# A fused four-layer kernel: the last block's second half in two quarters, their products on VectorE

## The reference

```python
x = x + L0(x)   # Haar transform, every level times one gate: v + gate * v for this kernel
x = x + L1(x)   # h_t = tanh(x_t Wx + b + h_{t-1} Wh), over 512 tokens
x = x + L2(x)   # below
x = x + L3(x)   # x + x @ (base + x_a x_b^T), x_a and x_b of rank 8 per batch row

# L2
forget_gate, input_gate = sigmoid(x Wf + bf), sigmoid(x Wi + bi)
gate_sum = forget_gate + input_gate + EPS
forget_norm, input_norm = forget_gate / gate_sum, input_gate / gate_sum
new_info = input_norm * (x Wh + bh)
log_cumprod = cumsum(log(forget_norm + EPS), axis=1)
scaling = exp(log_cumprod[:, -1:] - padded[:, :-1])      # product of the later forget factors
hidden = cumsum(scaling * new_info, axis=1) + exp(log_cumprod) * initial_hidden
```

## Time and profile before

| what | us |
|---|---|
| median of 3 runs | 1376.03 (1373.47 to 1377.22) |
| the profiled execution's own time | 1375.73 |
| its span in the profile | 1373.9 |
| TensorE busy | 1341.6 (98%) |
| VectorE busy | 1045.2 (76%) |
| GpSimd busy | 825.7 (60%) |
| ScalarE busy | 794.3 (58%) |

### The profile page before, as it was taken

How to read it: one execution, slowest core, us unless ns; L and a number is a source line. 1 busy time by engine, 2 the same in 40 slices (tenths; PEclk the granted TensorE clock), 3 DMA queues, 4 the chain that set the end, 5 groups by cost and what they waited for, 6 DMA issues and landing times. The chain is left out here.

```text
span 1373.9 us, 51170 instructions
## 1 busy us (share of the span) xinstructions
PE 1341.6 (98%) x21246; PEld 899.0 (65%) x21246; DVE 1045.2 (76%) x2694; ACT 794.3 (58%) x2733; POOL 825.7 (60%) x695
## 2 busy tenths in 40 slices
PE   8999999999999999999999999999999998998998
PEld 6656666666666666666666666666666645766776
DVE  5856878787878787878787878778777798894652
ACT  4387566666666666666666666666656543333342
POOL 3255656565756565656565656575647666775773
PEclk9999999999999999999999999999999999999999
DMA  9761141413131322232322314130305445677773
GB/s 372 279 256 37 26 72 25 72 28 69 33 64 35 62 41 57 41 56 42 56 51 47 60 38 70 27 56 10 61 6 110 113 89 158 227 210 237 265 250 118
DMA packets 304168, 134.74 MB, mean 98 GB/s; under 512 B 272945, under 2 KB 275121, under 8 KB 300738
## 3 DMA queue, kind: packets, MB, share of 16 engines
q1 hardware_dynamic: 303472, 131.10, 37.2%
q10 hardware_dynamic: 466, 0.38, 0.1%
HBM read 80.07 MB, written 51.38 MB: 96 GB/s over the span
## 5 line engine op out<-in xcount | busy, mean ns | idle before, releaser
L524 PEld LDWEIGHTS recb<-hs,scanS 128*128 128x128 f16 x16352 | 476.9, 96 | 137.1 <-DVE hs L1614 133.6
L524 PE MATMUL recb<-hs,scanS 128*128 128x32 f16 x16352 | 488.1, 176 | 4.3 <-DVE hs L1614 3.3
L792 ACT ACTIVATE hs<-pre 128x64 f16<-128x64 f32 x512 | 131.2, 256 | 387.9 <-DVE pre L1600 382.3
L1406 DVE RECIPROCAL gates<-gates 128x64 f32<-128x64 f32 x480 | 244.9, 531 | 0.0
L1600 DVE TENSOR_REDUCE pre<-recb 128x64 f32<-128x128 f32 x511 | 148.9, 291 | 123.1 <-PE recb L524 100.5
L1614 DVE TENSOR_TENSOR hs<-konst,hs 128x64 f16<-128x64 f32 x512 | 114.1, 223 | 105.8 <-ACT konst L793 105.4
L1114 POOL TENSOR_SCALAR hbuf<-hbuf,sup 128x512 f32<-128x512 f32 (+2 forms) x61 | 94.2, 1545 | 131.9 <-ACT hbuf L797 131.9
L1122 POOL TENSOR_TENSOR gates<-gates 128x512 f32<-128x512 f32 x60 | 76.4, 1273 | 87.7 <-DVE gates L1406 87.7
L797 ACT ACTIVATE hbuf<-pre 128x64 f32<-128x64 f32 x512 | 122.7, 240 | 0.0
L1256 POOL TENSOR_TENSOR x3l<-xt,x3h 128x512 fp32r<-128x512 f32 x64 | 83.7, 1309 | 57.9 <-ACT x3h L1004 57.9
L787 ACT ACTIVATE recb<-xw 128x128 f32<-128x128 f32 x447 | 116.9, 261 | 0.0
(11 more groups left out here) (283 smaller groups left out, 2882.3 us busy)
## 6 DMA issues: line engine op xcount, KB each, us to landing
xt<-in_x SPq DMA_DIRECT2D x64, 256.0 KB, 4.0
out<-scanS SPq DMA_DIRECT2D x63, 256.0 KB, 2.6
n_d<-nst SPq DMA_DIRECT2D x60, 256.0 KB, 3.1
x_d<-xt SPq DMA_DIRECT2D x60, 256.0 KB, 4.3
xt<-x_d SPq DMA_DIRECT2D x28, 512.0 KB, 5.7
stage<-in_w SPq DMA_DIRECT2D x11, 1024.0 KB, 7.0
xw<-n_d SPq DMA_DIRECT2D x14, 512.0 KB, 5.4
late<-n_d SPq DMA_DIRECT2D x14, 512.0 KB, 5.6
```

The source lines that it names most:

```text
L524: last = nc.tensor.matmul(sums[t % 2][:, m].rearrange("p a b -> p (a b)"), w[:, k, m * P:(m + 1) * P], hs[:, k].rearrange("p a b -> p (a b ...
L792: nc.scalar.activation(hs[:, :, 0, :], pre[t % 2][:], ACT.Tanh, scale=unscale).then_inc(s_h, 1)
L1406: nc.vector.reciprocal(piece, piece).then_inc(s_r, n)
```

## The change

1. Half 1 becomes two quarters: group 1 is batch rows 8 to 11, group 2 rows 12 to 15 (`group`, `side`), with instructions 128 elements wide (132 for scans). The reciprocal is one instruction for each.
2. The forget product and the product of share and suffix of both quarters are done by VectorE, directly behind the reciprocal and behind the scans. GpSimd keeps them for half 0 and keeps `add_half`.
3. The pieces stand at regular places: for group e + 1 and chunk m, shares after `hidden(8 + 16 e + 2 m)`, scans three places later, info six places later.
4. `spill_half` of group 2 stands at the end of b = 9, and the first load of row 12 behind the stores of row 9, with a wait for these spills.
5. ScalarE copies the whole candidate (512 wide, into xt's buffer of block 14) out of its bank before `last_X(3)`, and `last_info` reads it there for all groups. TensorE's first batch row waits for this copy alone and no longer for `last_info` of half 0.
6. The order at the start of the closing stage changes: `hidden(0)` and `hidden(1)` ahead of `following(2, 0)` and `decay_half(3, 0)`; `x3_low` interleaved with `times_n`; `x3_high` of row 1 ahead of `put_out(0)`.
7. `JOINED` is 2 instead of 1.
8. In block 1, at steps 9 and 10, two maxima (`greatest_x`) stand behind the step's `hs` instruction instead of ahead of it.

```diff
-JOINED = 1
+JOINED = 2
...
-REST = {5: [("sum", 0)], 6: [("rest", 0)], 7: [("sum", 1)], 8: [("rest", 1)], 9: [("sum", 2)], ...
+FIRST_REST = 8
+
+def rest_at(first, gap=2):
+
+    return {FIRST_REST + 16 * e + first + gap * m: (m, e + 1) for e in range(2) for m in range(C)}
+
+REST_SHARES, REST_SCANS, REST_INFO = rest_at(0), rest_at(3), rest_at(6)
+REST_FORGET, REST_TOTAL = rest_at(1), rest_at(4)
+REST_LATER = rest_at(7)
...
-        group = [slice(h * HALF, (h + 1) * HALF) for h in range(2)]
+        group = [slice(0, HALF), slice(HALF, HALF + B // 4), slice(HALF + B // 4, B)]
+        side = [slice(g.start * TS, g.stop * TS) for g in group]
...
                     elif m == 0:
                         pe.wait_ge(s_cb, t + 1)
-                        pe.wait_ge(s_n, final(t, 0))
...
             for k in range(C, SLOTS):
                 hidden(k)
...
+                if k in REST_SHARES:
+                    m, h = REST_SHARES[k]
+                    shares_of(m, h)
...
+                    nc.vector.tensor_tensor(flast[m][:, side[h]], flast[m][:, side[h]], rlast[m][:, side[h]], ALU.mult).then_inc(s_fr, 1)
+                if k in REST_SCANS:
...
+                    later(m, h)
+                    decay_half(m, h)
...
+                    nc.vector.tensor_tensor(share, share, sfx[:, m % 2, group[h], 1:SEG], ALU.mult).then_inc(s_vs, 1)
+                if k in REST_INFO:
+                    following(*REST_INFO[k])
+                    last_info(*REST_INFO[k])
```

More of the change, by code:

```diff
@@ L275, in rank, with scanned @@
             return h * C + m + 1
+        def scanned(m, h):
+            return 4 * C * (NBLK - 1) + rank(m, h) + (m + 1 if h == 0 else C)
         def final(m, h):
@@ L477, in _ @@
             for b in range(B):
-                if b + 2 < B and b + 2 != HALF:
+                if b + 2 < B and b + 2 not in (HALF, HALF + B // 4):
                     load("n", b + 2, 0)
@@ L1056, in _ @@
             last_n(2)
+            candidate(3)
             last_X(3)
-            candidate(3)
             x3_high(2)
@@ L1061, in _ @@
             x3_high(3)
+            x3_high(C)
             y_high(0)
-            x3_high(C)
+            x3_high(C + 1)
+            x3_high(C + 2)
             for t in range(NT):
                 put_out(0, t)
+            x3_high(C + 3)
             def high_and_rest(k):
@@ L1246, in times_n @@
                     loaded(pool, "n", k)
-                pool.wait_ge(s_F, rank(m, b // HALF))
+                pool.wait_ge(s_F, rank(m, next(h for h in range(3) if b < group[h].stop)))
                 part = nin[b % 2][:, m, 0:blocks * TS].rearrange("p (q t) -> p q t", t=TS)
@@ L1297, in _ @@
             add_half(2, 0)
-            times_n(2)
             x3_low(0)
             later_share(3, 0)
+            times_n(2)
+            x3_low(1)
             add_half(3, 0)
             times_n(3)
-            x3_low(1)
+            times_n(C)
             x3_low(2)
+            times_n(C + 1)
             x3_low(3)
-            for k in range(C, C + 3):
-                times_n(k)
+            times_n(C + 2)
             x3_low(C)
@@ L1631, in _ @@
                         factors(C - 1)
+                    if j == 1 and t in (9, 10):
+                        greatest_x(3, t - 7)
                     if j == 1 and t == 8:
@@ L1706, in later @@
                     dve.wait_ge(s_t, C * (last - 2) + m + 3)
-                for e in range(2):
-                    part = slice(h * HALF + e * B // 4, h * HALF + (e + 1) * B // 4)
+                for e in range(0, group[h].stop - group[h].start, B // 4):
+                    part = slice(group[h].start + e, group[h].start + e + B // 4)
                     dst, src = (s[:, part, :].rearrange("p b t -> p (b t)")[:, ::-1] for s in (sfx[:, m % 2], gst[:, m]))
@@ L1771, in _ @@
             decay_half(2, 0)
-            following(2, 0)
             hidden(0)
             later(3, 0)
+            last_info(1, 0)
+            following(2, 0)
+            hidden(1)
             decay_half(3, 0)
-            last_info(1, 0)
-            hidden(1)
+            last_info(2, 0)
             following(3, 0)
-            last_info(2, 0)
             hidden(2)
```

99 lines of the change are left out of this document (37 added, 62 removed).

## The result

The changed kernel takes 1379.89 us (median of 13 runs, 1377.01 to 1382.08), the kernel before 1376.06 beside it (13 runs): ratio 1.0024, 95% interval 1.0016 to 1.0033. By this ratio it is slower by about 3.3 us, 0.24%; the medians differ by 3.8. The forecast was 1376.5, "same". The profiled execution took 1380.9 us with a span of 1379.1, 5.2 more than the span of before.

A forecast was written before the change was run, and what follows sets the result against it. VectorE was taken to hold TensorE's rows 1 to 5, with about 23 us to win. Gains were given back: E8 0.5 us later and row 12 0.3 later, 0.8 on 1375.73, gave 1376.5 us; range 1363 to 1386.

The forecast's parts named there:

- x: Excess time of each VectorE instruction with two SBUF inputs, waiting for GpSimd's current instruction: 0.44 us whatever its width.
- E8: Start of batch row 8's low-rank matmuls on TensorE; forecast 1279.0 us against 1278.5 before, 0.5 later.
- Row 12's load: Row 12's first load waits in the queue as row 8's did; 0.3 us taken; rival of 4.6 + 2.9, chance 0.07.
- E9: Start of batch row 9's low-rank matmuls on TensorE; the prediction gave it no time of its own.
- the cheap lock: Rival: GpSimd is found busy less often, x below 0.36, measurably faster, 1366 us at x = 0.25; chance 0.32.
- The start: Closing stage's start: TensorE's third and fourth bank wait for ScalarE's candidate copies, winning 2.1 of 3.5 us.
- E0: Start of batch row 0's low-rank matmuls on TensorE; forecast 1153.7 us, before 1155.78.
- Row 3 and after: TensorE's rows 3 to 8 wait for VectorE: `hidden(15)` at 1191.2, `hidden(31)` at 1250.8, `hidden(35)` at 1267.7.
- E3: Start of batch row 3's low-rank matmuls on TensorE; forecast 1205.4 us, before 1204.6.
- E7: Start of batch row 7's low-rank matmuls on TensorE; forecast 1265.0 us, before 1265.73.
- The waits: Sign: TensorE waits about 10 us before row 3 and 5 before row 7, each with some 5 us of low clock behind.
- No wait near row 8's first load: Sign: that load's lateness lies under TensorE's 5.4 us wait for `hidden(31)`; before, it made TensorE wait 4.56 us.

The follow-up runs named there:

- row12: Changed kernel with the second quarter's stores one batch row earlier and row 12's first load ahead of factor loads and output stores in SyncE's queue: 1373.26 us, ratio 0.9982.
- pool_prod: Changed kernel with both products of the quarters on GpSimd, scans four and infos seven places behind the shares: 1373.44 us, ratio 0.9981 to the kernel before.
- pool_j8_cand: Changed kernel with quarter products on GpSimd, row 8's and 12's first loads ahead, `JOINED = 8`, and ScalarE's fourth candidate copy right behind the third: 1365.77 us, ratio 0.9929.
- spread: Changed kernel with the second quarter's VectorE work at every third place instead of every second: 1377.13 us, ratio 1.0004 to the kernel before.
- both_rows: row12 with row 8's first load also ahead of factor loads and stores in SyncE's queue: 1372.92 us, ratio 0.9972 to the kernel before.
- twice: row12 with eight extra VectorE products, each multiplying a reciprocal with itself, result unread: 1377.95 us, ratio 1.0020 to the kernel before.

## Why the prediction came out as it did

The number lay 3.4 us low, inside the range; the direction was right within the bound of 0.3%, but on its upper side. That it came so near is in part luck. The lock's price x was measured at 0.33, below the 0.36 where the prediction has the change measurably faster; by the sum's own steepness, 5.6 us for 0.1, it would have given about 1370. Steps that ran late, row 12 and the main loop made up for it. The sum ended at E8 0.5 later and row 12 0.3 later. Measured: E8 1.1 earlier from the memset, row 12 3.9 later, 0.17 in block 1. Times below are less 2.4 us, the main loop's part, which the sum counted at nothing; in the profiles the kernels with the new main loop reach the mark 1.7 us later on average.

- **Row 12's load: the term that failed.** "I take 0.3 us there, between 0 and 4.6 + 2.9" became 3.9, over half of the upper bound. The argument was "half as many bytes to spill". Bytes weren't it: the eight stores held the factor loads up by 1.2 us, while the load's place behind these, which wait for E9, and behind four more stores put its issue 6.6 us after E9. row12, with the stores a row earlier and the load ahead, removes it. The reason "half the bytes" was never compared with what stands in the queue.
- **x.** Forecast 0.44, measured 0.33 over 70 instructions; `hidden(8)` to `hidden(15)` took 31.6 us, not 33.8, `hidden(24)` to `hidden(31)` 30.4. This goes towards the cheap lock (x below 0.36), yet the time was not 1366: the steps that ran late took it. The 0.44 came from a stretch where GpSimd was busy 64.8 of 82 us; it was 56.4 here, and by that share alone x would be 0.38. That argument stood among the rival's, and I gave it no share in the central value. The share alone doesn't give x either: from `hidden(8)` to `hidden(35)` GpSimd was busy 0.69 of the time in the changed kernel and 0.81 in pool_prod, where the excess was 0.30. The estimate for an instruction that comes at a random moment, 0.47, is further off than 0.44.
- **The start.** E0 was to be 2.1 earlier. It came 0.9 later in the profiled execution and is at 50.6 to 50.8 in seven of the other kernels with this start, 0.5 earlier than before. The fourth bank waits 3.08 us for ScalarE: `last_n(2)`, ahead of that copy, waits for a `last_info` that now pays the lock too. pool_j8_cand shows that even 1.1 us here is worth nothing.
- **Rows 0 to 2.** 13.17 us a row, not 12.77; `hidden(8)` at 1160.2, not 1157.4. Two small misses against x.
- **Between the groups.** `hidden(15)` to `hidden(24)` took 28.0, not 25.8: a wait of 1.92 us for ScalarE's total at `following`, which no step had.
- **Row 3 and after.** `hidden(15)` 1191.8 (forecast 1191.2), E3 1205.9 (1205.4), `hidden(31)` 1250.2 (1250.8), E7 1264.1 (1265.0), `hidden(35)` 1265.9 (1267.7), E8 1277.4 (1279.0). The chain that the sum followed is the one that set row 8, and spread, both_rows and twice moved it by what was taken from or put on VectorE. The agreement up to `hidden(15)` is of two errors, the lock 2.2 too dear and `hidden(8)` 2.8 too early.
- **The waits.** 10 us at row 3 were 7.1, since row 2 ended later; 5 us ahead of row 7 were 2.62 for GpSimd and 1.80 for `hidden(31)`. "No wait near row 8's first load" was wrong in the profile (2.35 us on GpSimd) and nearly right for the time: with that load ahead, both_rows has E8 1.3 us earlier than row12.

Not settled: 2 us of the gap between the changed kernel and row12, and whether the main loop's later end belongs to the change.

## What to carry to other kernels

When a transfer waits for late stores, put its issue ahead of everything in the queue that isn't urgent, and price it by the issues that stand before it and by what those wait for, not by its bytes. Count a small instruction on a saturated VectorE by its own time and its share of the lock, and where GpSimd has idle time, leave the instruction there. After each gain look again for the next thing that comes in the same order as before: an earlier TensorE made row 12's wait longer (3.9, 4.1, 5.9 us lost at rows 10 and 11 in the changed kernel, spread and pool_prod).

## What the runs showed of the hardware

- The clock behind the same wait differs between executions. In the changed kernel TensorE waits 3.08 us at 1145.91 and then runs at 0.50, the level of 1.2 GHz (windows above). In spread it waits 3.10 us at the same place, and the clock is full:

```profile
1144.05:1146.05 2.00, 1.12 (x5) 0.94 (x6) 1.87 (x3) 1.06 (x5) 1.57 (x3) 1.00 0.38 62
1146.05:1148.05 2.00, 2.00 (x11) 1.63 (x10) 1.53 (x3) 0.86 (x3) 1.42 (x2) 1.00 1.05 155
```

  E0 is at 52.1 in the one and 49.6 in the other, 2.5 us apart by the clock, more than several of the terms of the sum. In row12, behind a wait of 3.10 us, the low stretch was about half as long, and E0 is at 50.8.
- VectorE's wait for the shared port is not proportional to the number of instructions: the doubled product raised the group's own durations by 0.63 us each and the chain by 0.42 (`hidden(8)` to `hidden(35)`, 104.6 to 108.0). Of the difference of 1.7 us, 1.0 are other waits of VectorE in that stretch that shrank (for ScalarE's total from 1.36 to 0.48 us, for GpSimd from 1.33 to 1.19).
